# Sequence part of a state-space and expert layer: block-end terms on GpSimd, wide polynomial steps, logits in parts, three vector states of sixteen, and a new order of the woven work

## The reference

```python
x_in, z = split(x @ in_proj_w.T + in_proj_b)
x_conv = silu(sum(x_pad[:, k:k + L] * conv_w[:, k] for k in range(4)) + conv_b)
x_dbl = x_conv @ x_proj_w.T                      # 64 for dt, 16 for B, 16 for C
dt = softplus(dt_low @ dt_proj_w.T + dt_proj_b)
A_bar = exp(dt * A)                              # per channel and state
h = A_bar * h + (A_bar - 1) / A * B * x_conv     # over the 2048 tokens
y = sum over states of h * C  +  D * x_conv
x = layernorm(x + (y * silu(z)) @ out_proj_w.T + out_proj_b)
router = sigmoid(x @ gate_w + gate_b)            # top 2 of 16 experts
```

## Time and profile before

| what | us |
|---|---|
| median of 3 runs (lowest to highest) | 3110.71 (3108.88 to 3116.9) |
| the profiled execution | 3114.07 |
| its span, first to last instruction | 3112.2 |
| busy: TensorE / VectorE / GpSimd / ScalarE | 2728.6 / 2513.6 / 2283.0 / 1787.5 |

### The profile page before, as it was taken

The page is one execution under the profiler, slowest core; times in us unless marked ns, Lnnn a source line. Parts: engine busy times, 40 slices in busy tenths (PEclk is TensorE's granted clock), DMA queues, the critical chain, the costliest instruction groups (busy, mean ns, idle before and its releaser), DMA issues. The chain is left out here.

```text
span 3112.2 us, 45625 instructions
## 1 busy us (share of the span) xinstructions
PE 2728.6 (88%) x10018; PEld 1567.4 (50%) x10019; DVE 2513.6 (81%) x3894; ACT 1787.5 (57%) x3543; POOL 2283.0 (73%) x1955
## 2 busy tenths in 40 slices
PE   6989898989999989899999999899989886899765
PEld 3445454545454545454544455454545454777543
DVE  5988888989798989898989897989797984555456
ACT  6575757575757575766666666575757541222222
POOL 2988888888787879797978887888787982000465
PEclk8999899999898999999999989999999886999887
DMA  2333333333333333333333333333333235555343
GB/s 85 105 108 104 100 112 94 115 92 114 96 111 100 112 95 115 93 114 98 112 97 108 103 103 103 105 99 112 95 114 97 97 101 214 169 175 169 115 125 118
DMA packets 241008, 349.65 MB, mean 112 GB/s; under 512 B 73303, under 2 KB 114267, under 8 KB 240220
## 3 DMA queue, kind: packets, MB, share of 16 engines
q1 hardware_dynamic: 225900, 304.17, 31.4%
q0 software_dynamic: 14832, 42.49, 4.1%
HBM read 288.36 MB, written 58.20 MB: 111 GB/s over the span
## 5 line engine op out<-in xcount | busy, mean ns | idle before, releaser
L611 POOL TENSOR_TENSOR hc<-h,c_rep 128x512 f32<-128x512 f32 x896 | 1134.4, 1271 | 302.8 <-DVE h L1146 131.0
L943 PE MATMUL y_ps<-hc,dg_inv 128*128 128x512 f32 x1792 | 953.1, 619 | 35.8 <-POOL hc L611 28.5
L1146 DVE TENSOR_TENSOR_SCAN h<-a_ps,carry,h 128x512 f32<-128x512 f32 x640 | 806.7, 1271 | 25.0 <-DVE skip L1182 7.6
L603 POOL TENSOR_TENSOR h<-x_conv,b_rep 128x512 f32<-128x512 f32 x640 | 820.8, 1283 | 3.3 <-ACT carry L699 3.3
L685 ACT ACTIVATE a_ps<-dt,a_mat 128x512 f32<-128x512 f32 x640 | 439.8, 688 | 589.0 <-DVE h L1146 551.0
L959 PEld LDWEIGHTS g_ps<-b_steps,x_conv_rows 128*128 128x128 f32 x3072 | 443.0, 210 | 325.8 <-issue 175.3
L943 PEld LDWEIGHTS y_ps<-hc,dg_inv 128*128 128x128 f32 x1792 | 323.8, 195 | 433.1 <-issue 283.4
L959 PE MATMUL g_ps<-b_steps,x_conv_rows 128*128 128x128 f32 x3072 | 455.8, 296 | 88.5 <-DVE carry L1162 73.4
L1115 DVE SCALAR_TENSOR_TENSOR h<-a_ps,h 128x512 f32<-128x512 f32 x640 | 428.1, 669 | 64.7 <-ACT a_ps L685 63.6
L1154 DVE TENSOR_TENSOR_SCAN h<-g_ps,carry,h 128x512 f32<-128x512 f32 x256 | 327.2, 1278 | 30.3 <-DVE g_ps L1139 25.8
L685 ACT ACTIVATE h<-dt,a_mat 128x512 f32<-128x512 f32 x384 | 271.6, 707 | 0.0
(11 more groups left out here) (247 smaller groups left out, 3946.4 us busy)
## 6 DMA issues: line engine op xcount, KB each, us to landing
c_rep<-bc_rows SPq DMA_DIRECT2D x512, 256.0 KB, 3.4
b_rep<-bc_rows SPq DMA_DIRECT2D x320, 256.0 KB, 3.7
gathered<-x_rows SPq DMA_DIRECT2D x144, 128.0 KB, 2.9
y_rows<-gathered SPq DMA_DIRECT2D x36, 512.0 KB, 3.1
x_t<-in_x_t SPq DMA_DIRECT2D x16, 512.0 KB, 6.0
x_tok<-in_x_tok SPq DMA_DIRECT2D x16, 512.0 KB, 4.8
out<-mixed_rows SPq DMA_DIRECT2D x16, 512.0 KB
x_t_rows<-y_gated SPq DMA_DIRECT2D x15, 512.0 KB, 5.0
```

Source lines behind the costliest of these rows:

```text
L603: nc.gpsimd.tensor_tensor(h[:, i % SLOTS, e], x_conv[:, u[1] % 2, chunk(i, e)], b_rep[:, n % BS], ALU.mult).then_inc(u_ready, 1)
L611: nc.gpsimd.tensor_tensor(hc[:, i % 2, e], h[:, i % SLOTS, e], c_rep[:, i % CS], ALU.mult).then_inc(hc_pool, 1)
L943: nc.tensor.matmul(y_ps[:, e], by, hc[:, i % 2, e], start=first_one, stop=(i % HALF == HALF - 1)).then_inc(summed, 1)
L1146: nc.vector.tensor_tensor_scan(slot, a_ps[:, e], slot, before_it, ALU.mult, ALU.add).then_inc(scanned, 1)
```

## The change

In the order of the diff:

- The logits `lg` are four parts (items 40 to 43) with one bias product for all, where they were one block with four bias products.
- The order of kinds is `ddfdfddfdfdddfdf` in place of `ddfddfdfddfddfdf`, and three states (4, 9, 15) in place of two (2, 10) have their product with C made by VectorE: 12 of 64 items in place of 8.
- Every list of places is new. Places that were formulas (the lead of `make_u`, `make_a`, `make_du`) are lists now. x0 begins at item 0 (it was 2), the scatters stand at items 1 to 15, the norm's sums at 20 and 22 (12 and 16), `x_tok` is loaded at SyncE's pair 8 (4), B is loaded six pairs ahead (four).
- `find_ends` goes to GpSimd at item 61. A copy with the sign turned (`turn_ends`, ScalarE, item 52) stands ahead of it.
- `make_both` goes to GpSimd at item 50.
- `softplus` makes a step for two chunks in one instruction of 1024 columns: four in place of eight.
- The split of the output bias at the start of the program has three instructions fewer.

```diff
-LOGS = 4 * FACTORS
+LOGS = 2 * FACTORS
+B_LEAD = 6
-KINDS = "ddfddfdfddfddfdf"
-BY_VECTOR = (2, 10)
+KINDS = "ddfdfddfdfdddfdf"
+BY_VECTOR = (4, 9, 15)
-        PLACE = [("d2", 0), ("d3", 1), ("x0", 2), ("x1", 4), ("o0", 6), ("o1", 10), ("c0", 14), ("c1", 18), ("r0", 22), ("r1", 23),
-                 ("x2", 24), ("x3", 26), ("t0", 28), ("t1", 29), ("T2", 30), ("T3", 31), ("c2", 32), ("c3", 36), ("lg", 40),
-                 ("z2", 41), ("low", 43), ("bc", 48), ("d0", 49), ("d1", 50), ("pf", 51), ("z3", 52), ("z0", 54), ("z1", 56),
-                 ("T0", 58), ("T1", 59), ("r2", 60), ("r3", 61)]
-        DU_AHEAD = {2: 2, 5: 2, 7: 2, 10: 2, 13: 2, 15: 2}
-        Z_AT = (51, 2)
-        SQUARES_AT = ((52, 53, 54), (3, 4, 5))
-        LOGS_AT = ((54, 55, 56, 57), (5, 6, 7, 8))
-        STEPS_AT = (50, 51, 53, 55, 59, 62)
+        PLACE = [("x0", 0), ("d3", 2), ("d2", 3), ("x1", 4), ("c0", 5), ("c1", 8), ("T2", 13), ("T3", 14), ("o0", 14), ("o1",
+                 18), ("x2", 20), ("r0", 23), ("r1", 27), ("c2", 29), ("x3", 30), ("c3", 35), ("r2", 38), ("t1", 39), ("t0", 39),
+                 ("r3", 40), ("lg", 40), ("low", 42), ("d0", 46), ("bc", 46), ("d1", 48), ("z1", 51), ("z2", 52), ("pf", 53),
+                 ("z3", 56), ("z0", 56), ("T1", 59), ("T0", 60)]
+        U_AT = [-5, -2, None, 4, None, 6, 8, None, 12, None, 15, 18, 20, None, 26, None, 29, 32, None, 34, None, 38, 41, None,
+                45, None, 47, 50, 51, None, 55, None]
+        A_AT = [-1, 1, 3, 4, 5, 7, 10, 12, 11, 13, 16, 18, 22, 20, 24, 25, 28, 31, 31, 36, 38, 39, 41, 42, 46, 45, 48, 53, 55,
+                56, 57, 58]
+        DU_AT = [None, None, 3, None, 5, None, None, 12, None, 14, None, None, None, 23, None, 29, None, None, 33, None, 37,
+                 None, None, 43, None, 47, None, None, None, 57, None, 59]
+        SCATTER_AT = (1, 2, 4, 7, 8, 12, 13, 15)
+        ADD_RELU_AT = (59, 60, 18, 20)
+        Z_AT = (49, 5)
+        STEPS_AT = (47, 48, 53, 55, 58, 63)
+        SUMS_AT = (20, 22)
+        SILU_AT = (15, 43)
+        SQUARES_AT = ((52, 53, 54), (5, 6, 13))
+        LOGS_AT = ((53, 57), (12, 16))
+        TURN_AT, ENDS_AT, BOTH_AT = 52, 61, 50
+        MAX_AT, INDEX_AT, IDS_AT, CHOOSE_AT, CANDIDATES_AT, REDUCE_AT, PLACES_AT, NOTED_AT = 45, 47, 49, 52, 55, 60, 61, 63
+        ROOT_AT, INVERSE_AT, NORMALISE_AT = 24, 26, 28
+        GATE_AT, HALO_IN_AT, HALO_OUT_AT = 58, 4, 47
+        SKIP_AT = (26, 29, 39, 41)
...
                 rows = bc_dram[n[1] % 2]
                 sp.dma_start(b_part[:], rows[ND:NS]).then_inc(parts_in, 16)
                 sp.dma_start(c_part[:], rows[NS + ND:]).then_inc(parts_in, 16)
-                wait(sp, ends_ready, count(n, 1, 0))
+                wait(sp, ends_turned, count(n, 1, 0))
...
+            def make_both(u, plan):
+
+                n = later(u)
+                pool.wait_ge(parts_in, count(n, 32, 32))
+                if plan is not first:
+                    emptied_all(pool, plan, u, [max("r2", "r3", key=ORDER.get)])
+                nc.gpsimd.tensor_tensor(both[0:NF], b_part[:], c_part[:], ALU.mult).then_inc(both_ready, 1)
+
+            def find_ends(u):
...
+                for c in range(CH):
+                    one = nc.gpsimd.tensor_tensor(minus_u[:, nq, c], b_minus[:], last_of[:, c].unsqueeze(1).to_broadcast([P, NF, TT]),
+                                                  ALU.mult)
+                one.then_inc(ends_ready, 1)
...
+            def turn_ends(u):
+
+                n = later(u)
+                act.wait_ge(ends_in, count(n, 16, 16))
+                wait(act, ends_ready, count(n, 1, 0))
+                nc.scalar.activation(b_minus[:], b_end[:, :, :, 1], ACT.Copy, scale=-1.0).then_inc(ends_turned, 1)
...
-                    emptied_all(pe, plan, u, ["t0", "t1"])
-                    for tt in range(TT):
-                        o = work[:, bank, tt * NE:(tt + 1) * NE]
-                        nc.tensor.matmul(o, ones[:], b_gate[:], start=True, stop=False)
-                        for k in range(KT):
-                            mm = nc.tensor.matmul(o, x1_t[:, k, tt * P:(tt + 1) * P], w_gate[:, k], start=False, stop=(k == KT - 1))
+                    logits = work[:, bank, 0:TT * NE].rearrange("p (t e) -> p t e", e=NE)
+                    if part == 0:
+                        emptied_all(pe, plan, u, ["t0", "t1"])
+                        nc.tensor.matmul(logits, ones[:], b_gate[:].unsqueeze(1).to_broadcast([1, TT, NE]), start=True, stop=False)
+                    for k in range(KT):
+                        mm = nc.tensor.matmul(logits[:, part], x1_t[:, k, part * P:(part + 1) * P], w_gate[:, k],
+                                              start=False, stop=(part == TT - 1 and k == KT - 1))
...
-                nc.vector.scalar_tensor_tensor(out=poly[:, half], in0=factor[:, half], scalar=ATANH[k][2], in1=other[:, half],
+                nc.vector.scalar_tensor_tensor(out=poly[:], in0=factor[:], scalar=ATANH[k][2], in1=other[:],
                                                op0=ALU.add, op1=ALU.mult).then_inc(softplus_step, 1)
```

More of the change, by code:

```diff
@@ L537, in _ @@
             load_parts((0, -1))
-            for i in range(4):
+            for i in range(B_LEAD):
                 if i < 2:
@@ L601, in make_u, with u_s_at @@
                     ou, oi = before(u, i, SLOTS)
-                    slot_free(pool, ou, oi)
+                    if on_pool(oi):
+                        carried_wait(pool, ou, oi)
+                ou, oi = before(u, i, SLOTS)
+                if on_pool(oi):
+                    hc_wait(pool, ou, oi, e)
+                else:
+                    wait(pool, scanned, count(ou, ITEMS, 2 * oi + e + 1))
                 nc.gpsimd.tensor_tensor(h[:, i % SLOTS, e], x_conv[:, u[1] % 2, chunk(i, e)], b_rep[:, n % BS],
                                         ALU.mult).then_inc(u_ready, 1)
+            U_PLACE = sorted((U_AT[i] + e, i, e) for i in range(PAIRS) for e in range(2) if plain(i))
+            def u_s_at(u, plan, m):
+                for at, i, e in U_PLACE:
+                    if at == m:
+                        make_u(u, i, e)
+                    if at == m - ITEMS and plan is not last:
+                        make_u(later(u), i, e)
             def make_hc(u, i, e):
@@ L627, in unit_program @@
                         make_hc(pu, pi, e)
-                    nu, ni = after(u, i, 2)
-                    if plain(ni) and not (plan is last and nu != u):
-                        make_u(nu, ni, e)
+                    u_s_at(u, plan, m)
                     if plan is not second and m == IDS_AT:
@@ L786, in squared @@
             def squared(n, g, k):
[L788 removed]
+                wait(act, softplus_step, count(n, LOGS, g * FACTORS))
                 if k == 0:
@@ L897, in unit_program @@
                         halo_wait(u, plan, m)
+                    if plan.has("pf") and m == NOTED_AT:
+                        act.wait_ge(route, count(later(u, -1), ROUTE, ROUTE))
                     a_s_at(u, plan, m)
@@ L1045, in weave @@
                     tile(u, plan, t, part)
-            DU_PLACE = [(2 * i + e - DU_AHEAD[i % HALF], i, e) for i in range(PAIRS) for e in range(2) if not plain(i)]
+            DU_PLACE = [(DU_AT[i] + e, i, e) for i in range(PAIRS) for e in range(2) if not plain(i)]
             def unit_program(u, plan):
@@ L1051, in unit_program @@
                     i, e = divmod(m, 2)
-                    pu, pi = before(u, i, 2)
-                    if not (plan is second and i < 2):
+                    pu, pi = before(u, i, LAG)
+                    if not (plan is second and i < LAG):
                         add_item(pu, pi, e)
@@ L1184, in make_skip @@
                 dve.nop().then_inc(emptied[bank], 1)
-            def make_both(u, plan):
-                n = later(u)
-                dve.wait_ge(parts_in, count(n, 32, 32))
-                if plan is not first:
-                    emptied_all(dve, plan, u, ["r3"])
-                else:
-                    dve.wait_ge(steps_ready, 3)
-                nc.vector.tensor_tensor(both[0:NF], b_part[:], c_part[:], ALU.mult).then_inc(both_ready, 1)
             def norm_so_far(pu, n):
@@ L1334, in _ @@
             whole(dve, unit_program)
+            if not on_pool(PAIRS - 1):
+                for e in range(2):
+                    make_hc((0, UNITS - 1), PAIRS - 1, e)
             for c in (CH - 2, CH - 1):
```

181 lines of the change are left out of this document (84 added, 97 removed).

## The result

The changed kernel takes 3143.34 us (median of 4 runs, 3139.91 to 3145.9), the kernel before 3112.55 beside it on the same chip: ratio 1.0082, 95% interval [1.0067, 1.0097]. It is slower by 0.8%, where 2930 us was forecast. The profiled span is 3138.0 us.

A forecast was written before the change was run, and what follows sets the result against it. VectorE was taken to set the pace. Own work -6.5 and waits -5.2 gave -11.7 us a unit, to 147.1; 177 us off in all, forecast 2930 us, range 2845 to 3025.

The forecast's parts named there:

- the placing of the waits: VectorE's waits, placed from the order lists as (a) to (d): 14.7 us a unit become 9.5, gain 5.2.
- (1): Four block-end products a unit leave VectorE for GpSimd: gain 4.67 us a unit.
- (2): The product for `both` leaves VectorE for GpSimd: gain 1.4 us a unit.
- (3): Softplus polynomial on VectorE, eight narrow steps become four wide: 11.2 to 7.6 us a unit, gain 3.6.
- rival D: Wide polynomial steps win nothing and block GpSimd for their length: time 3000 us; chance 0.26 together with rival B.
- (4): Twelve instead of eight products of state and C on VectorE, each with its carry: loss 3.2 us a unit.
- (a): At the logits, VectorE's wait for late factor products from TensorE falls from 9.8 to 1.5 us a unit: gain 8.3.
- (b): At the unit's head, x0 at item 0 asks for x_t before it lands: loss 3 us a unit.
- rival C: x_t late at the head alone delays TensorE, factor products and GpSimd: unit 160.3 us, time 3135; chance 0.06.
- (c): ScalarE at the sigmoid: 3 of VectorE's 4.9 us a unit of decay and poly waits stay, gain 1.9.
- (d): x_tok, loaded after later scatters, lands some 2 us late for the norm's first sum: loss 2 us a unit.
- rival B: Work goes but waits replace it, TensorE needing 144 us: unit 153, time 3025; chance 0.26 together with rival D.

The follow-up runs named there:

- e1: Changed kernel with the store of x1_t at SyncE's pair 21 in place of 16; ratio to the kernel before 0.9887, unit 156.7 us.
- e6: Kernel before the change with its x1_t store at SyncE's pair 10 in place of 16; ratio to the kernel before 1.0543, unit 170.4 us.
- e3: Changed kernel with the x1_t store at pair 21 and the next unit's first decay asked for two items earlier; ratio to the kernel before 0.9844, unit 155.5 us.
- e5: e3 with each wide polynomial step cut into two narrow ones; ratio to the kernel before 0.9822, unit 155.2 us.
- e9: e3 with two vector states (4, 9), the third (15) back on TensorE; ratio to the kernel before 0.9764, unit 155.3 us.
- f1: e3 with the polynomial covering only 128 of each 512 columns, the rest left uncomputed; ratio to the kernel before 0.979, unit 154.1 us.
- e8: e3 with block-end products and the product for both back on VectorE, items 62 and 63; ratio to the kernel before 0.9874, unit 156.0 us.
- g2: g1 with the softplus's sigmoid also replaced by an exponential of the same size; ratio to the kernel before 0.9586, unit 150.7 us.
- g1: e3 with the two SiLU activations replaced by copies of the same size; ratio to the kernel before 0.9761, unit 154.1 us.
- e7: e3 with the second SiLU at item 42 and the addition to spread given one SBUF input; ratio to the kernel before 0.984, unit 155.7 us.

## Why the prediction was wrong, by its steps

**The step that failed** is the placing of the waits: "Here I can only place them, unit by unit, from the order lists." It walked TensorE's, VectorE's, ScalarE's and GpSimd's lists; SyncE's only for x_tok and for `both`. The tiles `t0` and `t1` were moved by ten and eleven items, somebody waited for them in a list that wasn't moved along, and behind that waiter stood the load that GpSimd needs soon after. So a wait of GpSimd of 8.8 us a unit stood in no term. e1 and e6 show it: 3.5 of the 13.1 us a unit between forecast and result. The waits that the prediction named as signs of being wrong were others, and none came: `both` waits 5.6 us in thirteen units, the turned ends are not in the lists, and GpSimd waits 32.6 us for TensorE at the ring of hc, where it was 83.5. In all, 2.8 of the 13.1 us are own work that didn't leave (3.7 and not 6.5), and 10.2 are VectorE's idle time: 5.2 less was booked, 5.0 more came.

**The other failed step** is "So VectorE sets the pace" and with it the sum, which took VectorE's own work off the unit one for one. In e3's order 1 us of it is worth between nothing (e5, 1.0 us more busy) or 0.1 (e9, 2.7 less, with 4.8 more on GpSimd) and 0.5 us (f1). By that the 6.5 us of own work would be worth 3 at most, not 6.5. The 14.7 us of waits, some 5 of short waits and the 138.9 of work in the earlier trace rows add up to the unit, but they are exchanged for one another.

**Point by point.** (1) and (2): the work left VectorE as booked, and on GpSimd a block-end product takes 254 ns (0.3 taken). But it had stood at the loop's jump, where time is lost anyway (e8). (3): (74.8 + 48.0) / 16 = 7.7 us against 7.6 forecast; the price was right, but half of the gain came with the new order, in which narrow steps take 9.4 us and not 11.2 (e5), and its worth in time was nil. So rival D holds in its effect. Its mechanism, steps that block GpSimd for their length, isn't shown: with narrow steps GpSimd is busy for 1.0 us a unit less, and no run separates that from the rest. (4): the 192 products take 742 ns each, the carries 204, as taken; worth little for the same reason. Unforeseen: the addition to `spread`, from 457 ns to 2352, 1.9 us each time. The own work fell by 3.7 us and not by 6.5.
(a) g_ps: 127.3 to 47.9 us, 6.1 us a unit gained where 8.3 was booked; the mechanism held, part of the wait stays. (b) x_t at the head: TensorE waits 19.4 us in thirteen units, 1.5 each, where 3 were taken for VectorE; rival C is out by its size. (c) had the wrong sign: instead of 1.9 us gained, the decays cost 89.4 - 53.2 = 36.2 us more, 2.8 a unit, and the score 2.4 more. It also asked only what VectorE waits for behind the sigmoid: GpSimd's wait for the carries, 66.7 us where it was 2.6, is in no term. (d): no wait for x_tok appears in VectorE's larger rows; SyncE stands 79.1 us for the scatters, and nobody waits for it.
The time is near rival C's, 3135 (by its own terms 160.6 and not 160.3 us a unit), for another cause; rival B, "the work goes and waits come in its place", had the right shape and, at 153 us a unit, too small a price. After e3's two edits it is nearer: 155.5 us.

**Open.** What fixes the 150.7 us that g2 leaves, and why ten table loads are worth 4.8 us, the first six of them 1.4 and the next four 3.4. That the four loads of the sigmoid are the dear ones, by the decays and carries behind them, fits those rows but wasn't tried alone, and neither was putting the sigmoid back to items 51 and 2, where GpSimd hardly waited for carries. Why e9 gains before the third unit is open as well. So is how the 8.4 us a unit that still lie between the forecast and e3 divide among the moved places.

## What to carry to other kernels

When a producer is moved, list everyone who waits for it, the issuing queue above all, and read what stands behind each of these waiters: here a store that nobody was waiting for cost 1.9%. A busy engine is a bound only if taking work from it shortens the unit; one run that leaves a few microseconds of it out tells that before a plan is built on it, and here it gave half of each microsecond back. Where engines work in order with short rings of buffers between them, look also at the long stretches of an engine with a lower share (here a sigmoid between two table loads on ScalarE), and at all who wait behind them.

## What the runs showed of the hardware

- The jump at a loop's end shows as up to 5.1 us of idle time without a releaser on VectorE (25.5 us in 6 jumps). With 4.2 us of VectorE work just ahead it is 2.0 us in all, and without the SiLU loads on ScalarE (g1) 4.9; asking for the decay earlier leaves 21.2. What it consists of stays open.
- A polynomial step of a quarter of the width is not four times shorter. Groups by line of f1, VectorE, thirteen units:
```profile
L1292 DVE SCALAR_TENSOR_TENSOR poly<-poly,x_arg 128x256 f32<-128x256 f32 x26 | 46.1, 1774 | 3.4 <-ACT poly L854 3.4
L1292 DVE SCALAR_TENSOR_TENSOR poly<-square,poly 128x256 f32<-128x256 f32 x26 | 20.7, 795 | 0.0
```
  With 1024 columns they took 2550 and 1483 ns in e3. So 768 columns are worth 0.7 to 0.8 us, and the first step takes 1 us more than the second at the same width.
- An addition of 4 columns on VectorE took 0.46 us on average before, 2.35 after, 2.62 with one SBUF input (e7) and 3.36 in g2. A product of 24 columns takes 0.92 us (e8) to 1.22 (before) on VectorE, 0.18 at the shortest, and 0.25 on GpSimd. In the traces the long additions end 0.02 to 0.04 us after the end of a GpSimd product (734.35 after 734.33 in e3), and so do the four block-end products of the kernel before, by 0.06: 837.43 after 837.37, 679.46 after 679.39. That fits a wait of these instructions for GpSimd's, longer than one product of 1.27 us. No run took GpSimd's products away beside them, so the cause isn't shown.
